# A vision tower on one Trainium2 core: scale and mean of the last norm folded into the head's weight, the patches load in two halves, the wide layer's products by operand, and image 0's 192-channel attention steps first

## The reference

```python
x = einsum('bchpwq,dcpq->bhwd', patches, conv_w)          # 256 tokens x 128 per image
for i in range(2):                                        # two layers of width 128
    y = ln(x) * ln1_g[i] + ln1_b[i]
    q, k, v = split(y @ qkv_w[i])                         # 8 heads of 64
    q = softmax(q, axis=-1) * scale; k = softmax(k, axis=-2)
    x = x + (q @ (k.T @ v)) @ out_w[i] + out_b[i]
    y = ln(x) * ln2_g[i] + ln2_b[i]
    x = x + gelu(y @ ff1_w[i] + ff1_b[i]) @ ff2_w[i] + ff2_b[i]
h = (ln(x) * lnf_g + lnf_b) @ head_w + head_b             # 256 x 192: the head
# a second stage on 192 channels: linear attention, 12 heads of 16
q, k, v = split(ln(h) @ W_qkv);  q = elu(q) + 1;  k = elu(k) + 1
z = 1 / (q @ sum(k) + 1e-6)
h = h + ((q @ (k.T @ v)) * z) @ W_out + b_out
# a third: a wide layer with 768 hidden units, weights mixed by masks
out = h + new_gelu(ln(h) @ w_fc.T + b_fc) @ w_proj.T + b_proj
```

## Time and profile before

| | us |
|---|---|
| runs | 126.94, 126.92, 126.31 |
| median | 126.92 |
| the profiled execution | 126.33 |
| its span, first to last instruction | 124.5 |

### The profile page before, as it was taken

One profiled execution on the slowest core, in us unless ns is written; L12 is line 12 of the kernel. 1 busy time (PEld: TensorE's weight loads), 2 busy tenths in 40 slices (PEclk: granted clock), 3 DMA queues, 4 the chain that ended last, 5 costly groups with the idle time before them and its releaser, 6 DMA issues.

```text
span 124.5 us, 2213 instructions
## 1 busy us (share of the span) xinstructions
PE 115.0 (92%) x830; PEld 99.3 (80%) x830; DVE 77.3 (62%) x243; ACT 63.2 (51%) x150; POOL 45.4 (36%) x56
## 2 busy tenths in 40 slices
PE   6999899999999999998999899897989988999990
PEld 6999899956797799996766789785777867998990
DVE  5200474988877775688999869649486665335001
ACT  4010352755876683658765859165854456232520
POOL 0000104053999622227669667465140050050000
DMA  4999998999600000000000000000000000000101
GB/s 110 350 425 432 388 417 283 372 417 417 207 5 0 3 0 5 0 0 0 0 0 0 5 0 0 3 0 5 0 0 0 0 0 5 0 0 9 54 0 63
DMA packets 4003, 12.37 MB, mean 99 GB/s; under 512 B 457, under 2 KB 1946, under 8 KB 3738
## 3 DMA queue, kind: packets, MB, share of 16 engines
q1 hardware_dynamic: 3946, 12.20, 26.1%
q10 hardware_dynamic: 48, 0.05, 0.1%
HBM read 11.85 MB, written 0.39 MB: 98 GB/s over the span
## 4 chain that ended last, share of the span: by engine, by line
PE 64%; DVE 14%; DMA 9%; ACT 4%; issue 3%; POOL 2%; SPq 2%; ACTq 0%
DMA patches_sb<-in_patches 9%; PE bank L421 6%; PE bank L517 6%; PE bank L328 6%; PE bank L440 5%; PE bank L414 3%; PE bank L397 3%; PE bank L362 3%; PE bank L392 3%; PE bank L374 2%; PE bank L428 2%; PE bank L503 2%; PE bank L350 2%; SPq L270 2%; PE bank L406 2%
## 5 line engine op out<-in xcount | busy, mean ns | idle before, releaser
L1826 POOL TENSOR_TENSOR rstd<-mv,minus_half 128x2 f32<-128x2 f32 x14 | 9.9, 710 | 46.4 <-DVE mv L949 46.4
L1844 POOL TENSOR_TENSOR qn<-q,rqsum 128x512 f32<-128x512 f32 x8 | 8.4, 1044 | 9.8 <-DVE rqsum L1019 9.8
L1607 ACT ACTIVATE patches_sb<-bank,fcb 128x256 f32<-128x256 f32 x12 | 5.1, 471 | 10.6 <-PE bank L514 10.6
L1570 ACT ACTIVATE kexp<-bank,nkmax 128x256 f32<-128x256 f32 x16 | 7.5, 472 | 5.3 <-DVE nkmax L999 5.3
L421 PEld LDWEIGHTS bank<-cw,qT 128*128 128x128 f32 x64 | 8.0, 191 | 2.4 <-issue 1.5
L421 PE MATMUL bank<-cw,qT 128*128 128x128 f32 x64 | 8.9, 280 | 0.7 <-DVE x L1034 0.4
L517 PE MATMUL bank<-projw,patches_sb 128*128 128x192 f32 x48 | 9.4, 332 | 0.0
L440 PE MATMUL bank<-restw,hid 128*128 128x128 f32 x64 | 8.8, 281 | 0.1
L1586 ACT ACTIVATE hid<-bank,small_sb 128x256 f32<-128x256 f32 x16 | 6.5, 474 | 3.7 <-PE bank L435 3.6
L440 PEld LDWEIGHTS bank<-restw,hid 128*128 128x128 f32 x64 | 7.8, 191 | 0.6 <-issue 0.3
L328 PEld LDWEIGHTS bank<-embed_sb 128*128 128x128 f32 x60 | 7.9, 211 | 0.2
(11 more groups left out here) (165 smaller groups left out, 325.3 us busy)
## 6 DMA issues: line engine op xcount, KB each, us to landing
embed_sb<-in_embed SPq DMA_DIRECT2D x3, 768.0 KB, 7.9
patches_sb<-in_patches SPq DMA_DIRECT2D x2, 1024.0 KB, 12.6
restw<-in_rest_w SPq DMA_DIRECT2D x2, 768.0 KB, 15.4
qkvw<-in_qkv_w SPq DMA_DIRECT2D x3, 256.0 KB, 11.2
qkvw<-in_qkv_w SPq DMA_DIRECT2D x1, 768.0 KB, 15.2
...
```

Source lines behind the costliest of these rows:

```text
L1570: return nc.scalar.activation(kexp[:, c, :], K_BANK[s][c // 2][:, (c % 2) * TOKENS:(c % 2 + 1) * TOKENS], ACT.Exp, bias=nkmax[i][:, c:c + ...
L1826: return nc.gpsimd.tensor_tensor(rstd[i][:], mv[i][:, :, 1], minus_half[:], ALU.pow)
L1844: return nc.gpsimd.tensor_tensor(qn[:, t, :].rearrange("p (h d) -> p h d", h=HEADS), q[:, t, :].rearrange("p (h d) -> p h d", h=HEADS), rq ...
```

## The change

*Patches.* patches1a is loaded by two DMAs of four chunks each; TensorE waits for the second in front of `conv(1, 4, 6)`.

*Head's weight.* ScalarE scales the rows of head_w by lnf_g early on (`head_gain`), TensorE multiplies the result with a matrix of 1/128 to get its column means on all partitions (`head_weight_means`, behind `head_offset`), and VectorE subtracts them (`centre_head_weight`, ahead of the last `ff_low_part`). The product of x with this weight is that of the centred x. So `centre` and `centred_last` go, TensorE turns x itself behind `x_new`, and ScalarE's `gain` becomes a plain `evict`.

*By operand.* The product by the rest tile becomes a stage of its own between "high" and "low". For keys and queries, and for image 0's first two chunks of the wide layer, the stages of two blocks are interleaved. Some banks are given out anew so that both blocks can be open.

*Order.* On VectorE image 0's split comes ahead of image 1's last moments, both `head_rows` and moments of image 1 come ahead of image 0's `phi3_max`, and later image 0's attention comes ahead of image 1's low part and maxima. On ScalarE image 1's eviction for the head comes ahead of image 0's exponential, and image 0's attention eviction ahead of image 1's exponentials. `add_attention3(0, 0)` waits for its own half only.

The core of the diff:

```diff
-        TURN4_BANK = [bank[3], bank[5]]
+        TURN4_BANK = [bank[7], bank[5]]
...
-        ATT3_BANK = [bank[2], bank[7]]
+        ATT3_BANK = [(bank[2], bank[6]), (bank[7], bank[7])]
...
-        FC3_BANK = [(bank[3], bank[2], bank[6]), (bank[5], bank[0], bank[0])]
+        FC3_BANK = [(bank[3], bank[2], bank[4], bank[2], bank[6], bank[2]), (bank[5], bank[5], bank[0], bank[0], bank[0], bank[0])]
+        FC3_HALF = [(0, 0, 0, 1, 0, 0), (0, 1, 0, 1, 0, 1)]
...
-            load_patches(0, 8, "patches1a")
+            load_patches(0, 4, "patches1a")
+            load_patches(4, 8, "patches1c")
...
+            def head_weight_means():
+
+                return nc.tensor.matmul(HROW_BANK[:, E:2 * E], one_over_d[:], headw_gain[:], start=True, stop=True)
...
+                if "rest" in stages:
+                    nc.tensor.matmul(dst, yT3_rest[i][:, tile], aqkvw_parts[0][:, 1, at], start=False, stop=False)
+                    mm = nc.tensor.matmul(dst, yT3_rest[i][:, tile], aqkvw_parts[1][:, 1, at], start=False, stop=False)
                 if "low" in stages:
-                    nc.tensor.matmul(dst, yT3_lo[i][:, tile], aqkvw_parts[0][:, 0, at], start=False, stop=False)
-                    nc.tensor.matmul(dst, yT3_rest[i][:, tile], aqkvw_parts[0][:, 1, at], start=False, stop=False)
-                    mm = nc.tensor.matmul(dst, yT3_rest[i][:, tile], aqkvw_parts[1][:, 1, at], start=False, stop=True)
+                    mm = nc.tensor.matmul(dst, yT3_lo[i][:, tile], aqkvw_parts[0][:, 0, at], start=False, stop=True)
...
+            def fc3_high(i, c):
+                at = slice(c * P, (c + 1) * P)
+                for part in range(2):
+                    mm = nc.tensor.matmul(fc3_out(i, c), fcw_parts[part][:, 0, at], yT3_hi[i][:],
+                                          start=(part == 0), stop=False)
+                return mm
+
+            def fc3_rest(i, c):
+                at = slice(c * P, (c + 1) * P)
+                for part in range(2):
+                    mm = nc.tensor.matmul(fc3_out(i, c), fcw_parts[part][:, 1, at], yT3_rest[i][:],
+                                          start=False, stop=False)
+                return mm
+
+            def fc3_low(i, c):
+                at = slice(c * P, (c + 1) * P)
+                return nc.tensor.matmul(fc3_out(i, c), fcw_parts[0][:, 0, at], yT3_lo[i][:], start=False, stop=True)
+
             def fc3(i, c):
-                at = slice(c * P, (c + 1) * P)
-                dst = FC3_BANK[i][c // 2][:, (c % 2) * TOKENS:(c % 2 + 1) * TOKENS]
-                nc.tensor.matmul(dst, fcw_parts[0][:, 0, at], yT3_hi[i][:], start=True, stop=False)
-                nc.tensor.matmul(dst, fcw_parts[1][:, 0, at], yT3_hi[i][:], start=False, stop=False)
-                nc.tensor.matmul(dst, fcw_parts[0][:, 0, at], yT3_lo[i][:], start=False, stop=False)
-                nc.tensor.matmul(dst, fcw_parts[0][:, 1, at], yT3_rest[i][:], start=False, stop=False)
-                return nc.tensor.matmul(dst, fcw_parts[1][:, 1, at], yT3_rest[i][:], start=False, stop=True)
+                fc3_high(i, c)
+                fc3_rest(i, c)
+                return fc3_low(i, c)
...
             pe.wait_ge(loaded["patches1a"], 16)
             conv(1, 0, 2)
             conv(1, 2, 4)
+            pe.wait_ge(loaded["patches1c"], 16)
             conv(1, 4, 6)
...
             head_offset()
+            pe.wait_ge(head_weight_gain, 1)
+            head_weight_means()
...
-            pe.wait_ge(centred_last, 2)
-            turn(TURNF_BANK[0], xn[0]).then_inc(last_turned, 1)
+            pe.wait_ge(x_new, 6)
+            turn(TURNF_BANK[0], x[0]).then_inc(last_turned, 1)
...
+            pe.wait_ge(x_new, 8)
+            turn(TURNF_BANK[1], x[1]).then_inc(last_turned, 1)
             pe.wait_ge(high3, 1)
             qk3_high(0, 0)
             qk3_high(0, 1)
+            pe.wait_ge(rest_low3, 1)
+            qk3_rest(0, 0)
             pe.wait_ge(low3, 1)
             qk3_low(0, 0).then_inc(qk3_done, 1)
-            pe.wait_ge(centred_last, 4)
-            turn(TURNF_BANK[1], xn[1]).then_inc(last_turned, 1)
+            qk3_rest(0, 1)
             qk3_low(0, 1).then_inc(qk3_done, 1)
...
+            qk3_high(1, 1)
+            pe.wait_ge(rest_low3, 2)
+            qk3_rest(1, 0)
+            qk3_rest(1, 1)
+            pe.wait_ge(attention3_ready, 2)
+            turn_heads(AT3_BANK[0], att3[0]).then_inc(attention3_turned, 1)
             pe.wait_ge(low3, 2)
             qk3_low(1, 0).then_inc(qk3_done, 1)
-            qk3_high(1, 1)
-            pe.wait_ge(attention3_ready, 2)
-            turn_heads(AT3_BANK[0], att3[0]).then_inc(attention3_turned, 1)
             qk3_low(1, 1).then_inc(qk3_done, 1)
...
+            pe.wait_ge(h_mid, 2)
...
+            pe.wait_ge(high4, 1)
+            fc3_high(0, 0)
+            fc3_high(0, 1)
+            pe.wait_ge(rest_low4, 1)
+            fc3_rest(0, 0)
+            fc3_rest(0, 1)
             pe.wait_ge(low4, 1)
-            fc3(0, 0).then_inc(fc3_done, 1)
-            fc3(0, 1).then_inc(fc3_done, 1)
+            fc3_low(0, 0).then_inc(fc3_done, 1)
+            fc3_low(0, 1).then_inc(fc3_done, 1)
+            fc3(0, 2).then_inc(fc3_done, 1)
             pe.wait_ge(attention3_ready, 4)
             turn_heads(AT3_BANK[1], att3[1]).then_inc(attention3_turned, 1)
-            fc3(0, 2).then_inc(fc3_done, 1)
...
+            def centre_head_weight():
+                return nc.vector.tensor_tensor(headw_centred[:], headw_gain[:], HROW_BANK[:, E:2 * E], ALU.subtract)
...
-            dve.wait_ge(mean_last_ready, 1)
-            centre(0, 0, x, D).then_inc(centred_last, 1)
-            dve.wait_ge(mean_last_ready, 2)
-            centre(0, 1, x, D).then_inc(centred_last, 1)
...
-            def gain(i, bankof):
-                return nc.scalar.activation(yT[i], bankof[:, 0:TOKENS], ACT.Copy, scale=col("lnf_g"))
+            def head_gain():
+                return nc.scalar.activation(headw_gain[:], headw[:], ACT.Copy, scale=col("lnf_g"))
```

95 lines of the change are left out of this document (55 added, 40 removed).

## The result

| | before | after |
|---|---|---|
| runs, us | 126.94, 126.92, 126.31, 126.42 | 124.62, 124.91, 125.55, 124.75 |
| median, us | 126.67 | 124.83 |
| profiled execution / its span | 126.33 / 124.5 | 124.62 / 122.8 |

The ratio is 0.9862, with a 95% interval from 0.9813 to 0.9912: faster beyond the noise, by 1.8 us or 1.4%. 125.5 had been said, in a range of 124.7 to 126.8; 124.83 lies in this range, and just under the 124.9 at which the forecast's own range (without the rivals) ended.

The account below looks back on a forecast made before the run. TensorE was taken to set the end, with 64% of the chain. Terms -0.35 + 0.33 - 0.88 - 0.38 = -1.28 us made the profiled execution 125.05 and the median 125.64, stated as 125.5 us, range 124.7 to 126.8.

Parts of the forecast that it names:

- rival (2): Patches loads: the split brings nothing, the later patches landing with their later issue; 125.85 us, chance 12%.
- (a): TensorE, image 0's key and query blocks: first ends at 87.36 in place of 87.56, second 0.5 us earlier.
- (b): ScalarE: image 1's eviction goes ahead of the table load; first exponential starts at 87.40 in place of 87.60.
- (c): VectorE: image 1's head rows and moments precede image 0's maxima; key and query transposition stays at 90.9, nothing won.
- (d): Image 0's attention precedes image 1's low part; output projection starts at 96.52 in place of 96.89, -0.37 us.
- (e): Image 1's exponentials pay: its transposition starts 0.5 us later, at 99.9, hidden as its context still starts at 100.38.
- (f): Image 0's sum, moments and deviation 0.5 us earlier; next transposition starts at 101.19 in place of 101.42, -0.23 us.
- Wide layer: TensorE works through the 0.50 us gap; image 1's projection at 105.73 after 0.4 idle, -0.38 us including the order's steps.
- (1): End of the kernel: engine queues slip by a few tenths each and the tail's 0.38 us is lost; 125.9 us, 15%.
- (3): Both (1) and (2) happen, or half of the head norm's 0.88 us goes too; 126.3 us, 11%.
- (4): ScalarE: the table load is followed by another 1.28 us, exponential at 88.7; 126.1 us, chance 3%.
- (5): TensorE's clock falls after longer idle time; four microseconds of slowed work give 129.5 us, chance 5%.

Follow-up runs that it names:

- a_maxima_first: The kernel after with VectorE taking image 0's two maxima ahead of image 1's moments: 47.00 us from head's offset to end, in place of 47.67 to 47.73.

## Why the prediction was right, and where it was not

The sum was -1.28 us; between the two profiled executions it was 126.33 - 124.62 = 1.71. Term by term, in starts of TensorE rows, where the shift in front of each is taken out:

| term | predicted | trace | by experiment |
|---|---|---|---|
| split patches | -0.35 | -0.47 (72.66 to 72.19) | medians -0.18, 0.00, -0.10 in three pairs; up to 1.57 waited for the next load |
| product for the means | +0.33 | +0.03 | +0.03 up to the head, and +0.33 for a second |
| head's norm | -0.88 | -0.88 | -0.85 up to the head, -0.95 to the end, with the product |
| order and wide layer | -0.38 | -0.39 | -0.23 on top of the head's norm, +0.75 without |
| sum | -1.28 | -1.71 | -1.18 in the stretch, which has no patches in it |

*Split patches: the mechanism failed at its second half, though the trace of after came out near it.* The first half's wait did go. The step that failed is "with a backlog of 14 us an issue half a microsecond later should not land later", on which the value -0.35 stood in place of the other bound, +0.05. The other patches were there at 20.7 to 22.6 us with the split and at 20.5 to 21.1 without, and before's own case (6.7 + 14.1 = 20.8, needed at 21.26) had only 0.46 us to spare. Whatever is won ahead of this wait is lost at it in many executions, and the profile of after happened to be one where the load came just in time. What the split is worth stays open: the three pairs of medians (-0.18, 0.00, -0.10) and the median start of the head's offset (-0.07) lie nearer to rival (2) than to -0.35, but the times alone exclude neither. The DMA row of the page stands at 8 or 9 in nearly all slices until the load ends, so a load with an issue more ahead of it would be expected later; that this is what delayed it, no run shows. The Trainium skill (Perfetto Trace Analysis, section DMA Optimizations) says that splitting a load may help if the DMA engines are generally idle. Here they were not, and no gain clear of the noise was measured.

*The product: the term was mis-sized, by 0.30 us, beyond its own lower bound of 0.16.* The step "in the middle of a run without gaps" read the idle column, in which a wait of 0.18 us lies under the modelled end of the product. The two starts, 72.66 and 73.17, were there to read: 0.51 us for two passes that are 0.33 long.

*The head's norm: right*, by the trace to the hundredth (head at 81.75 before, 80.43 after: 1.32 earlier, of which 0.44 was there at the transposition in the feed-forward, 74.17 and 73.73). That the next wait, for GpSimd's inverse deviation, wouldn't take over held too: behind the head VectorE's idle time ends with TensorE's product.

*The order's steps*, with the 1.32 added to after's times. (a) The first block ends at 87.37, 87.36 was said; the second 0.47 earlier than before, 0.5 was said. (b) The exponential right behind the load: 86.08 + 1.32 = 87.40, as said. (c) The second maximum ends at 90.84, 90.85 was said; the transposition starts at 90.89: nothing won, as said, and a_maxima_first shows it from the other side. (d) The projection at 96.49, 96.52 was said. (e) Image 1's transposition at 99.78, 99.9 was said; its context at 100.26 and so 0.12 earlier than said. The transposition waits 0.63 us for VectorE (98.46 in after): the sign of being wrong "a wait over 0.6 us before image 1's context" is met by a hair, one row ahead of the context, but this wait is the later start that (e) itself gives and calls hidden. (f) The next transposition at 101.20, 101.19 was said. Wide layer: image 1's projection at 105.65 after an idle 0.35, 105.73 and 0.4 were said.

What I hadn't seen is that these steps hold together. The order costs 0.75 us where the head is not shortened first, and gives 0.23 where it is; the effects of the two parts alone, -0.95 and +0.75, make -0.20, and together they gave -1.18. The working for (c) had image 1's head end at 88.5, and by the traces that takes both parts: image 1's head starts 6.85 us behind image 0's in before, 6.76 with the norm alone, 7.05 with the order alone, and 5.97 with both; so the sum was right, but "-0.38" is not a price at which the order could be bought singly; "-0.88" nearly is (-0.95 alone).

*The median.* 125.5 is 0.45 above the 125.05 of the profiled execution, for before's median of three runs lay 0.59 above its own. After's median came out 0.21 above its profiled execution. These 0.24 us and the trace's 0.43 (1.71 - 1.28) are the 0.67 between 125.5 and 124.83. The 1.8 us were luck in part, and mostly luck of the four runs of before: their median is 126.67, while the four later sets of 11 to 17 runs of the same kernel had 126.20 to 126.42, and after's two medians are 124.83 and 124.97. Measured again, the gain was 126.24 - 124.97 = 1.27 by the medians and 1.36 by the ratio, against 1.28 predicted. That this is so close is luck too: -0.35, of which the medians show -0.18, 0.00 and -0.10, and +0.33, of which 0.03 came, cancel.

*Rivals.* (1) did not happen. (2): open, see above. (3), both or half of the 0.88 gone too: no, the 0.88 came in full. (4): the load of 1.28 us at 84.74 ends at 86.02 and the exponential starts at 86.08. The Trainium skill (ScalarE: Activation LUTs, section What ACT_TABLE_LOAD costs) has a drain of about 1.38 us behind each load; this trace shows 0.06. (5): the granted clock is full over the whole span, through 1.27 us of idle time at 88.3 to 89.6, and the four passes behind it take 0.64 us as before. No run here shows the lower level in this stretch. The Trainium skill (TensorE: Matmul & The Clock Gate, section What's actually happening) lets idleness bring the clock down; an idle time of 1.3 us did not do it here.
